# Packed steps of a fused four-layer block: probabilities turned by VectorE and through memory instead of by TensorE

## The chip, the cores and the metric

The program runs on one core of a Trainium2 chip. The core has five engines with a queue of their own each: TensorE (PE, matrix products; its weight loads are listed as PEld), VectorE (DVE), ScalarE (ACT), GpSimd (POOL) and SyncE (SP), which here only issues transfers. Engines wait for one another through semaphores, and each runs its instructions strictly in the order written. The metric is the device time in microseconds of one execution; lower is better.

## The reference

Four layers act on x (4 batches of 512 rows of 512), with a context of 4 x 512 x 256:

```
x = x + tanh(g_xattn[0]) * L0_xattn(layernorm(x), ctx)    # one head, softmax of q k^T over 512 keys
x = x + tanh(g_ffn[0])   * L0_ffn(layernorm(x))           # one 512 x 512 layer, weights from bits
x = x + tanh(g_xattn[1]) * L1_xattn(layernorm(x), ctx)    # 16 heads of 128
x = x + tanh(g_ffn[1])   * L1_ffn(layernorm(x))           # 16 experts, each row goes to 4

L1_xattn:  q = rmsnorm(h @ Wq)   k = rmsnorm(c @ Wk)   v = c @ Wv         (per head)
           out = softmax(q k^T / sqrt(128)) @ v ;  result = concat(out) @ Wo
L1_ffn:    for every expert: down( silu(gate(x)) * up(x) ), weighted by topk_weight
```

## The kernel before

**Precision.** Every product is made of three: each operand is split into a rounded part (`_hi`) and the rest (`_lo`), and lo x hi, hi x hi and hi x lo are added up in one PSUM bank (`product`, L505 to L507). Each split costs a ScalarE cast (`copy_hi`) and a subtraction on VectorE or GpSimd (`lower`).

**The steps.** After a first part (layers L0, up to about 150 us) the kernel runs steps t = 0 to 65. There are 64 items, each a (head, batch) of L1_xattn: first the 16 heads of batch 0, then for each head batches 1 to 3. Step t works on three items at a time: it projects keys, values and queries of item t, makes scores and probabilities of item u = t-1, and values and output projection of item w = t-2. When batch 0 is through its attention, its expert layer runs as 31 blocks of 128 rows (b = t - 20). Steps 20 to 50 carry one block each beside their attention work: these are the **packed** steps. A block needs three weight chunks: gate and up in two halves of 704 KB (`gate_up_weights`) and down in 768 KB (`down_weights`).

**Probabilities.** The four score tiles of an item (128 queries x 512 keys each) lie in two score banks by turns. VectorE takes the row maximum (`maximum`), scales it (`shift`), ScalarE takes the exponential into `prob` (`softmax`). The product with the values needs keys on the partitions, so each tile is turned: four TensorE transposes with the identity (`probs`, L573), into PSUM, then a cast (`probs_hi`) and a subtraction (`probs_lo`) write `probT`.

**Orders.** Nothing is scheduled by a program: each engine's `step(t)` is a list of calls in order. SP's list of a packed step is: second gate-up chunk (waits until the down product of the block before is through), store of that block's result, down chunk (waits for `gate_up(0)`), the weights of the next head if there is one (two steps in three), then the expert number of the next block by a load into a register, and that block's first gate-up chunk (waits for `gate_up(1)`).

```
for t in range(NI + 2):                       # SP
    ...
    if 0 <= b < NB - 1:
        e = expert(b + 1)
        gate_up_weights(b + 1, 0, e)          # first work of ScalarE in step t+1
```

## Time and profile before

| | us |
|---|---|
| three runs | 1462.48, 1463.65, 1465.13 (median 1463.65) |
| profiled execution, span from first to last instruction | 1461.5 |
| what lies around the span (median less span) | 2.15 |
| one packed step (PE's turn of `h_row`: 93 transposes, 3 a step, from 509.9 to 1214.6 us) | about 23.5 |
| PE busy | 1437.8 (98%) |
| DVE, ACT, POOL busy | 1107.0, 977.5, 864.5 |
| packets of the DMA queues | 55495, 142.74 MB, mean 98 GB/s |

The profiled execution has no time of its own in the record beside its span; the median stands for it. A packed step is read off by windows of 23.48 us that begin at the first score product (581.87, 605.35, 628.83 us).

### The profile page before, as it was taken

What the parts mean: (1) busy time and instruction counts of PE and PEld (TensorE: products, weight loads), DVE (VectorE), ACT (ScalarE), POOL (GpSimd) and SP (SyncE); (2) the same over time, 40 slices, a digit from 0 to 9 for tenths busy, and PEclk for the clock granted to TensorE, in tenths of its full rate; (3) what the DMA queues carried; (4) which work ended last, traced back from release to release, by engine and by line L of the source; (5) the groups of instructions that cost most, each with busy time, mean ns of one, the idle gap of its engine ahead of it and who ended that gap; (6) DMA issues with size and microseconds to landing.
All of it is one profiled execution on the core that took longest, in us unless ns stands there. A gap on an engine that the chain in (4) does not pass through costs nothing.

```text
span 1461.5 us, 23763 instructions
## 1 busy us (share of the span) xinstructions
PE 1437.8 (98%) x8086; PEld 1223.0 (84%) x8086; DVE 1107.0 (76%) x2100; ACT 977.5 (67%) x2224; POOL 864.5 (59%) x701
## 2 busy tenths in 40 slices
PE   8999999999999999999999999999999999999998
PEld 6778788888888888888888888888888888888887
DVE  7888777777777777777777777777777776787777
ACT  7864477777776667667676767667676765666664
POOL 4785555555554566666575757575666655664341
PEclk9999999999999999999999999999999999999999
DMA  8420011111111333434333433433434331321002
GB/s 325 159 66 16 22 44 45 57 44 44 44 44 44 139 124 126 149 108 147 124 129 127 139 123 127 139 117 132 136 115 144 125 126 36 107 82 37 8 1 87
DMA packets 55495, 142.74 MB, mean 98 GB/s; under 512 B 5392, under 2 KB 5392, under 8 KB 55376
## 3 DMA queue, kind: packets, MB, share of 16 engines
q1 hardware_dynamic: 51616, 128.90, 26.1%
q0 software_dynamic: 3760, 12.32, 3.0%
q8 instruction: 66, 1.08, 0.3%
q14 instruction: 53, 0.43, 0.1%
HBM read 126.79 MB, written 14.42 MB: 97 GB/s over the span
## 4 chain that ended last, share of the span: by engine, by line
PE 82%; DVE 7%; ACT 4%; POOL 4%; issue 2%; DMA 0%; ACTq 0%; SPq 0%; DVEq 0%; POOLq 0%
PE w_bank L505 10%; PE w_bank L507 10%; PE w_bank L506 10%; PE j_bank L505 9%; PE j_bank L507 9%; PE j_bank L506 9%; PE t_bank L573 7%; PE s_bank L505 4%; PE s_bank L507 4%; PE s_bank L506 4%; PE t_bank L538 2%; POOL q_scale L1855 2%; POOL wo_lo L1815 2%; ACT prob L927 1%; PE t_bank L657 1%
## 5 line engine op out<-in xcount | busy, mean ns | idle before, releaser
L927 ACT ACTIVATE prob<-s_bank,neg_bias,q_scale 128x512 f32<-128x512 f32 x255 | 198.0, 777 | 186.5 <-DVE neg_bias L1422 186.4
L1262 DVE TENSOR_TENSOR probT_lo<-t_bank,probT_hi 128x512 fp32r<-128x512 f32 x260 | 176.4, 689 | 168.4 <-ACT probT_hi L892 168.4
L1476 DVE SCALAR_TENSOR_TENSOR x_sb<-w_bank,inv_sum,x_sb 128x512 f32<-128x512 f32 x254 | 188.4, 744 | 0.0
L1401 DVE TENSOR_REDUCE neg_max<-s_bank 128x1 f32<-128x512 f32 x255 | 168.6, 682 | 0.9 <-PE s_bank L507 0.9
L1815 POOL TENSOR_TENSOR xnT_lo<-xnT_raw,xnT_hi 128x512 fp32r<-128x512 f32 (+2 forms) x47 | 126.5, 2693 | 61.5 <-ACT xnT_hi L892 61.5
L573 PE MATMUL t_bank<-ident,prob 128*128 128x128 f32 x1008 | 151.4, 273 | 1.3 <-ACT prob L927 1.1
L892 ACT CAST probT_hi<-t_bank 128x512 fp32r<-128x512 f32 x260 | 150.1, 590 | 1.8 <-PE t_bank L515 1.8
L1855 POOL TENSOR_TENSOR q_scale<-q_ss,minus_half 128x4 f32<-128x4 f32 x64 | 65.9, 1030 | 143.6 <-DVE q_ss L1414 143.6
L505 PE MATMUL j_bank<-wkv_lo,cT_hi 128*128 128x256 f32 x512 | 145.1, 283 | 0.7 <-DVE oT_lo L1262 0.4
L507 PE MATMUL j_bank<-wkv_hi,cT_lo 128*128 128x256 f32 x512 | 144.6, 282 | 0.0
L506 PE MATMUL j_bank<-wkv_hi,cT_hi 128*128 128x256 f32 x512 | 144.4, 282 | 0.0
L1815 POOL TENSOR_TENSOR sqs_lo<-xn,sqs_hi 128x512 fp32r<-128x512 f32 x62 | 80.6, 1300 | 104.2 <-ACT xn L1007 104.2
L1815 POOL TENSOR_TENSOR cT_round<-cT_raw,x_round 128x1408 fp32r<-128x1408 f32 (+1 forms) x31 | 104.5, 3371 | 58.8 <-ACT x_round L892 58.8
L573 PEld LDWEIGHTS t_bank<-ident,prob 128*128 128x128 f32 x1008 | 121.6, 140 | 20.9 <-ACT prob L927 2.6
L505 PE MATMUL w_bank<-wo_lo,oT_hi 128*128 128x512 f32 x254 | 112.5, 443 | 2.6 <-POOL wo_lo L1815 0.4
L892 ACT CAST oT_hi<-j_bank 128x512 fp32r<-128x512 f32 x64 | 37.0, 578 | 113.2 <-PE j_bank L507 113.2
L505 PE MATMUL s_bank<-kv_lo,qT_hi 128*128 128x512 f32 x255 | 110.1, 432 | 0.3 <-DVE kv_lo L1496 0.2
L505 PE MATMUL j_bank<-xnT_lo,wq_hi 128*128 128x512 f32 x256 | 108.5, 424 | 0.0
L505 PEld LDWEIGHTS j_bank<-wkv_lo,cT_hi 128*128 128x128 f32 x512 | 97.3, 190 | 9.3 <-DVE oT_lo L1262 3.6
L507 PE MATMUL j_bank<-xnT_hi,wq_lo 128*128 128x512 f32 x256 | 101.1, 395 | 0.0
L506 PEld LDWEIGHTS j_bank<-wkv_hi,cT_hi 128*128 128x128 f32 x512 | 97.4, 190 | 4.3
L507 PE MATMUL s_bank<-kv_hi,qT_lo 128*128 128x512 f32 x255 | 100.6, 395 | 0.0
(308 smaller groups left out, 4454.2 us busy)
## 6 DMA issues: line engine op xcount, KB each, us to landing
stage<-w SPq DMA_DIRECT2D x96, 256.0 KB, 3.4
xnT_raw<-w_gu SPq DMA_DIRECT2D x31, 704.0 KB, 4.8
cT_raw<-w_gu SPq DMA_DIRECT2D x31, 704.0 KB, 4.7
xnT_raw<-w_dn SPq DMA_DIRECT2D x16, 768.0 KB, 4.4
cT_raw<-w_dn SPq DMA_DIRECT2D x15, 768.0 KB, 4.7
planes<-bits SPq DMA_DIRECT2D x16, 512.0 KB, 4.8
y<-stage SPq DMA_DIRECT2D x31, 256.0 KB, 4.0
x_sb<-x SPq DMA_DIRECT2D x5, 1024.0 KB, 10.9
```

The lines of the kernel that those rows point to most:

```text
L505: pe.matmul(dst, lh, rl, start=first, stop=False)
L506: pe.matmul(dst, lh, rh, start=False, stop=False)
L507: return pe.matmul(dst, ll, rh, start=False, stop=last)
L538: last = pe.transpose(t_bank[0][:, j * P:(j + 1) * P], kv_raw[:, j, 0:HD], ident[:])
L573: last = pe.transpose(prob_bank(t, i)[:, j * P:(j + 1) * P], prob[:, i, j * P:(j + 1) * P], ident[:])
L892: return nc.scalar.copy(dst, src)
L927: nc.scalar.activation(prob[:, i, :], score_bank(t, i)[:], ACT.Exp, bias=neg_bias[:, u % 2, i:i + 1], scale=q_scale[:, u % 2, i:i + 1], ac ...
L1262: return nc.vector.tensor_tensor(dst, src, hi, ALU.subtract)
L1401: nc.vector.tensor_reduce(neg_max[:, u % 2, i:i + 1], score_bank(t, i)[:], AX_X, ALU.max, negate=True).then_inc(own_max, 1)
L1476: nc.vector.scalar_tensor_tensor(out=here, in0=w_bank[0][:] if packed else out_bank(t, i)[:], scalar=inv_sum[:, w % 2, i:i + 1], in1=here, ...
L1815: return nc.gpsimd.tensor_tensor(dst, src, hi, ALU.subtract)
L1855: nc.gpsimd.tensor_tensor(q_scale[:, u % 2, :], q_ss[:, u % 2, :], minus_half[:], ALU.pow).then_inc(q_scale_ready, 1)
```

## The change

In the packed steps (and only there: `moved(u)`) TensorE no longer turns the probabilities. Instead, for each pair of tiles (128 x 1024):

- ScalarE writes the exponentials in blocks of 32 keys (`rearrange("p (r j c) -> p j r c")`);
- VectorE transposes every 32 x 32 block in place (`turn_quads`, one instruction for a pair);
- SP stores the pair to device memory (512 KB in runs of 2 KB), waits for the store, and loads it back with four transfers of 128 KB, each onto 32 partitions, in runs of 512 bytes (`move_pair`);
- ScalarE casts (`moved_hi`) and VectorE subtracts (`moved_lo`) 128 x 1024 from SBUF to SBUF instead of four times 128 x 512 from PSUM.

Pair 0 is split at the end of the step, pair 1 at the head of the next. The third score tile gets a bank of its own (t_bank[1]), and the orders of all engines in a packed step are new. In all steps `probT` lies in another order (query blocks of 32 by key tiles), which the value products read with a two-level pattern.

```diff
+            def move_pair(u, pair):                                   # SP
+                if not moved(u):
+                    return
+                sp.wait_ge(p_quads[pair], MOVES[u] + 1)
+                wait(sp, p_moved[pair], 16 * NT * MOVES[u])
+                sp.dma_start(turn_dram[pair].rearrange("i p m -> p i m"), prob_pair(pair)).then_inc(p_stored[pair], 16)
+                sp.wait_ge(p_stored[pair], 16 * (MOVES[u] + 1))
+                for c in range(NT):
+                    sp.dma_start(
+                        prob_pair(pair)[c * QUAD:(c + 1) * QUAD].rearrange("a i (r m) -> a (i r) m", r=NT),
+                        turn_dram[pair].rearrange("i (r a) (c m) -> c a (i r) m", r=NT, c=NT)[c]).then_inc(
+                            p_moved[pair], 16)
...
                 if t >= H + 2 and fresh(t - 2):
                     out_weights(SET[t - 2] + 1)
+                move_pair(t - 1, 0)
+                move_pair(t - 1, 1)
                 if 0 <= b < NB - 1:
                     e = expert(b + 1)
                     gate_up_weights(b + 1, 0, e)
...
                 def values():                                         # PE
-                    need(pe, p_lo, 4, w, 4)
+                    wait(pe, p_lo, TILES[w + 1])
+                    if moved(w):
+                        pe.wait_ge(pair_lo[0], MOVES[w + 1])
+                        pe.wait_ge(pair_lo[1], MOVES[w + 1])
...
+                def moved_hi(v, pair):                                # ACT
+                    if not moved(v):
+                        return
+                    act.wait_ge(p_moved[pair], 16 * NT * (MOVES[v] + 1))
+                    need(act, pv_mm, 1, v - 1, 1)
+                    copy_hi(probT_pair(0, pair), prob_pair(pair)).then_inc(pair_hi[pair], 1)
...
                 gate_up_hi(0)
                 rows_to_hi()
+                moved_hi(w, 1)
...
+                    moved_hi(u, 0)
+                    query_squares()
+                    return
...
+                def turn_quads(pair):                                 # DVE
+                    if not moved(u):
+                        return
+                    need(dve, p_exp, 4, u, 2 * pair + 2)
+                    both = prob_pair(pair).rearrange("p i s -> p (i s)")
+                    nc.vector.transpose(both, both).then_inc(p_quads[pair], 1)
+
+                def moved_lo(v, pair):
+                    if not moved(v):
+                        return
+                    dve.wait_ge(pair_hi[pair], MOVES[v] + 1)
+                    lower(probT_pair(1, pair), prob_pair(pair), f32(probT_pair(0, pair))).then_inc(pair_lo[pair], 1)
...
+                    query_lo()
+                    key_lo()
+                    add(2)
+                    inner_lo()
+                    moved_lo(u, 0)
+                    add(3)
+                    return
```

SP, one packed step from the store of the last block's result to the next block's first chunk. `turn` is the new buffer in device memory, `block_expert` the table of expert numbers. Before:

```order
L447 DMA y<-stage 128x512 [waits y_copied]
L442 ISA [waits a_mm]
L442 DMA cT_raw<-w_dn 128x2x768
L411 DMA stage<-w 128x512 [waits wo_lo]
L427 TENSOR_LOAD block_expert
L427 ISA x2
L437 ISA [waits b_mm]
L437 DMA xnT_raw<-w_gu 128x1408
```

And now, from the down chunk on:

```order
L496 DMA xnT_raw<-w_dn 128x1536
L451 DMA stage<-w 128x512 [waits wo_lo]
L472 DMA turn<-prob 128x2x512 [waits p_moved0,p_quads0]
L475 DMA prob<-turn 32x8x128 [waits p_stored0]
L475 DMA prob<-turn 32x8x128 x3
L472 DMA turn<-prob 128x2x512 [waits p_moved1,p_quads1]
L475 DMA prob<-turn 32x8x128 [waits p_stored1]
L475 DMA prob<-turn 32x8x128 x3
L481 TENSOR_LOAD block_expert
L481 ISA x2
L491 ISA [waits b_mm]
L491 DMA cT_raw<-w_gu 128x2x704
```

Between the head's weights and the next block's expert number stand ten more transfers and four more waits, two of them for stores to land.

ScalarE, from the end of a packed step to the exponentials of the next. `xnT_raw` or `x_round` here hold a gate-up chunk, `routes` the inner rows of the block. Before:

```order
L892 CAST routes<-w_bank 128x384 [waits d_mm,h_turned]
L1005 ACTIVATE sqs_hi<-j_bank 128x512 [waits q_ss_mm,q_lo]
L1007 ACTIVATE xn<-j_bank 128x512 [waits q_ss_out]
L892 CAST probT_hi<-t_bank 128x4x128 [waits p_turned]
L892 CAST xnT_hi<-xnT_raw 128x1408 [waits a_in]
L892 CAST xnT_hi<-w_bank 128x512 [waits b_mm,q_mm,rows_mm]
L892 CAST wo_hi<-stage 128x512 [waits w_mm,wo_in]
L892 CAST oT_hi<-j_bank 128x512 [waits w_mm,pv_mm]
L927 ACTIVATE prob,row_sum<-s_bank,neg_bias,q_scale 128x512 [waits p_turned,s_max] x2
```

And now:

```order
L967 CAST routes<-w_bank 128x384 [waits d_mm,h_turned]
L967 CAST probT_hi<-prob 128x1024 [waits pv_mm,p_moved0]
L1095 ACTIVATE sqs_hi<-j_bank 128x512 [waits q_ss_mm,q_lo]
L1097 ACTIVATE xn<-j_bank 128x512 [waits q_ss_out]
L967 CAST xnT_hi<-xnT_raw 128x1408 [waits a_in]
L967 CAST xnT_hi<-w_bank 128x512 [waits b_mm,q_mm,rows_mm]
L967 CAST probT_hi<-prob 128x1024 [waits pv_mm,p_moved1]
L967 CAST wo_hi<-stage 128x512 [waits w_mm,wo_in]
L967 CAST oT_hi<-j_bank 128x512 [waits w_mm,pv_mm]
L1009 ACTIVATE prob,row_sum<-s_bank,neg_bias,q_scale 128x4x4x32 [waits pair_lo0,s_max] x2
```

The cast of the first gate-up chunk (`waits a_in`) still opens the step, and the new cast of pair 1 stands behind it.

VectorE, the end of a packed step. Before:

```order
L1496 SCALAR_TENSOR_TENSOR kv_lo<-t_bank,gain,kv_hi 128x512 [waits kT_hi]
L1476 SCALAR_TENSOR_TENSOR x_sb<-w_bank,inv_sum,x_sb 128x512 [waits w_mm]
L1262 TENSOR_TENSOR qT_lo<-j_bank,qT_hi 128x512 [waits q_hi]
L1262 TENSOR_TENSOR routes<-w_bank,routes 128x384 [waits h_hi]
L1476 SCALAR_TENSOR_TENSOR x_sb<-w_bank,inv_sum,x_sb 128x512 [waits w_mm]
L1262 TENSOR_TENSOR probT_lo<-t_bank,probT_hi 128x4x128 [waits p_hi]
```

And now:

```order
L1352 TENSOR_TENSOR qT_lo<-j_bank,qT_hi 128x512 [waits q_hi]
L1600 SCALAR_TENSOR_TENSOR kv_lo<-t_bank,gain,kv_hi 128x512 [waits kT_hi]
L1580 SCALAR_TENSOR_TENSOR x_sb<-w_bank,inv_sum,x_sb 128x512 [waits w_mm]
L1352 TENSOR_TENSOR routes<-w_bank,routes 128x384 [waits h_hi]
L1352 TENSOR_TENSOR probT_lo<-prob,probT_hi 128x1024 [waits pair_hi0]
L1580 SCALAR_TENSOR_TENSOR x_sb<-w_bank,inv_sum,x_sb 128x512 [waits w_mm]
```

The addition of the third output tile now comes behind both the query's and the key's low part, and the subtraction of pair 0 stands ahead of the last addition.

## Rows read from the trace of the kernel before

**Rows 1.** The page's busy times of all engines (us, share of the span, instructions).
```profile
PE 1437.8 (98%) x8086; PEld 1223.0 (84%) x8086; DVE 1107.0 (76%) x2100; ACT 977.5 (67%) x2224; POOL 864.5 (59%) x701
```
**Rows 2.** Window of one step: length, busy time of PE, PEld, DVE, ACT, POOL, granted clock, DMA share, GB/s.
```profile
581.87:605.35 23.48, 23.48 (x138) 20.60 (x138) 17.42 (x33) 16.17 (x36) 14.84 (x10) 1.00 0.38 126
```
**Rows 3.** The chain of waits, 580 to 640 us: start, length in us, engine and tile.
```profile
592.60 0.44 PE t_bank L573 x4
...
604.28 0.44 PE t_bank L573 x4
```
**Rows 4.** Timeline of PE: start, length, line, operation; values, gate-up, first turn.
```profile
586.37 0.39 PE L505 MATMUL j_bank<-probT_lo,kv_hi 128*128 128x512 f32 x1
590.52 0.33 PE L505 MATMUL w_bank<-xnT_lo,xnT_hi 128*128 128x352 f32 x1
592.43 0.60 PE L573 MATMUL t_bank<-ident,prob 128*128 128x128 f32 x4
```
**Rows 5.** Timeline of SP, its issues in and just ahead of packed steps.
```profile
480.21 0.38 SPq L469 DMA_DIRECT2D rows<-x_sb  x1
481.75 0.36 SPq L437 DMA_DIRECT2D xnT_raw<-w_gu  x1
592.77 0.34 SPq L442 DMA_DIRECT2D xnT_raw<-w_dn  x1
601.61 0.55 SPq L437 DMA_DIRECT2D cT_raw<-w_gu  x1
616.84 1.07 SPq L411 DMA_DIRECT2D stage<-w  x2
```
**Rows 6.** DMA issues (KB each, us to landing); windows from 457, 586 and 608 us.
```profile
x<-x_sb SPq DMA_DIRECT2D x1, 1024.0 KB, 4.3
stage<-w SPq DMA_DIRECT2D x1, 256.0 KB, 2.7
cT_raw<-w_gu SPq DMA_DIRECT2D x1, 704.0 KB, 4.8
y<-stage SPq DMA_DIRECT2D x1, 256.0 KB, 6.0
```
**Rows 7.** Timeline of ACT: chunk cast, row cast, value cast, first exponential of the step.
```profile
583.29 1.39 ACT L892 CAST xnT_hi<-xnT_raw 128x1408 fp32r<-128x1408 f32 x1
584.57 0.60 ACT L892 CAST xnT_hi<-w_bank 128x512 fp32r<-128x512 f32 x1
589.29 0.59 ACT L892 CAST oT_hi<-j_bank 128x512 fp32r<-128x512 f32 x1 [3.60 <-PE j_bank L507]
590.81 0.78 ACT L927 ACTIVATE prob<-s_bank,neg_bias,q_scale 128x512 f32<-128x512 f32 x1 [0.93 <-DVE neg_bias L1422]
```
**Rows 8.** Timelines of DVE and POOL: two-input operations on SBUF, alone and side by side.
```profile
41.75 0.74 DVE L1788 SCALAR_TENSOR_TENSOR kv_raw<-stage,bit_w,kv_raw 128x512 f32<-128x512 f32 x1
46.39 2.35 DVE L1788 SCALAR_TENSOR_TENSOR kv_raw<-stage,bit_w,kv_raw 128x512 f32<-128x512 f32 x1
585.25 1.61 DVE L1262 TENSOR_TENSOR xnT_lo<-xnT_raw,xnT_hi 128x1408 fp32r<-128x1408 f32 x1
45.77 2.42 POOL L1815 TENSOR_TENSOR cT_lo<-x_sb,cT_hi 128x1024 fp32r<-128x1024 f32 x1
601.82 3.51 POOL L1815 TENSOR_TENSOR xnT_lo<-xnT_raw,xnT_hi 128x1536 fp32r<-128x1536 f32 x1
```
**Rows 9.** Windows of 1 us around a pause of PE, columns as in rows 2.
```profile
50.00:51.00 1.00, 0.00 (x0) 0.00 (x0) 0.82 (x2) 1.00 (x5) 0.92 (x2) 1.00 0.77 289
52.00:53.00 1.00, 1.00 (x5) 0.77 (x4) 0.00 (x0) 0.90 (x1) 1.00 (x1) 0.61 0.00 0
53.00:54.00 1.00, 1.00 (x4) 0.81 (x3) 0.90 (x1) 0.00 (x0) 1.00 (x2) 0.50 0.03 10
54.00:55.00 1.00, 1.00 (x3) 0.79 (x3) 1.00 (x2) 0.12 (x1) 1.00 (x2) 0.50 0.68 240
55.00:56.00 1.00, 1.00 (x4) 0.77 (x3) 0.97 (x2) 1.00 (x2) 1.00 (x2) 0.68 0.93 289
```

More of the change, by code:

```diff
@@ L123, with moved, turned_tiles, flamingo_kernel @@
 LAST = {b: max(t for t in range(NI) if ITEMS[t][1] == b) for b in range(B)}
-def flamingo_kernel(nc, x, xT, ctxT, vecs, w0, bits, w1, w_gu, w_dn, topk_idx, topk_w, x0_dram, rows_dram, y_dram, out):
+QUAD = 32
+def moved(u):
+    return T0 <= u + 1 < T0 + NB
+def turned_tiles(u):
+    return () if moved(u) else range(NT)
+TILES = [sum(len(turned_tiles(v)) for v in range(u)) for u in range(NI + 1)]
+MOVES = [sum(moved(v) for v in range(u)) for u in range(NI + 1)]
+def flamingo_kernel(nc, x, xT, ctxT, vecs, w0, bits, w1, w_gu, w_dn, topk_idx, topk_w, x0_dram, rows_dram, y_dram, turn_dram, out):
     x_tiles = x.rearrange("(b i p) d -> b p i d", b=B, p=P)
@@ L320, in flamingo_kernel @@
             sem("s_mm"), sem("s_max"), sem("p_exp"), sem("p_turned"), sem("p_hi"), sem("p_lo"))
+        p_quads, p_stored, p_moved, pair_hi, pair_lo = (
+            [sem(f"{name}{pair}") for pair in range(2)] for name in ("p_quads", "p_stored", "p_moved", "pair_hi", "pair_lo"))
         late_normed, late_turned, late_hi, late_lo = (
@@ L534, in turn_keys @@
                     need(pe, q_ss_out, 1, 0, 1)
+                elif moved(t - 1):
+                    need(pe, q_ss_out, 1, t - 1, 1)
                 elif t:
-                    need(pe, p_lo, 4, t - 1, 2)
+                    wait(pe, p_lo, TILES[t - 1] + 2)
                 for j in range(NT):
@@ L556, in scores @@
                         need(pe, kT_lo, 1, u, 1)
-                    need(pe, p_exp, 4, u, (0, 0, 0, 1)[i] if t == LAST_SCORES else i - 1)
+                    if moved(u):
+                        need(pe, p_exp, 4, u, (0 if moved(u - 1) else -1, 0, 0, 1)[i])
+                        if i == 2 and not moved(u - 1):
+                            wait(pe, p_lo, TILES[u])
+                    elif moved(u - 1):
+                        need(pe, p_exp, 4, u, max(i - 1, 0))
+                    else:
+                        need(pe, p_exp, 4, u, (0, 0, 0, 1)[i] if t == LAST_SCORES else i - 1)
                     product(score_bank(t, i)[:], [a[:, u % 2, i * P:(i + 1) * P] for a in qT],
@@ L661, in table @@
                     pe.wait_ge(place_ready, 1 + NT)
-                    need(pe, p_lo, 4, 0, 4)
+                    wait(pe, p_lo, TILES[1])
                     for c in range(PAIRS):
@@ L793, in step @@
                 gate_up(0)
+                if moved(u):
+                    scores(3)
+                    key_value(1)
+                    project_out(0)
+                    query((0, 1))
+                    project_out(1)
+                    gate_up(1)
+                    query((2, 3))
+                    key_turn()
+                    project_out(2)
+                    turn_inner()
+                    project_out(3)
+                    return
                 probs(0)
@@ L925, in softmax @@
                     need(act, s_max, 4, u, i + 1)
[L926 to L927 removed]
+                    if i in turned_tiles(u - 1):
+                        wait(act, p_turned, TILES[max(u - 1, 0)] + list(turned_tiles(u - 1)).index(i) + 1 if u else 0)
+                    else:
+                        act.wait_ge(pair_lo[i // 2], MOVES[u])
+                    dst, src = prob[:, i, :], score_bank(t, i)[:]
+                    if i not in turned_tiles(u):
+                        dst = dst.rearrange("p (r j c) -> p j r c", j=NT, c=QUAD)
+                        src = bank_keys(score_bank(t, i))
+                    nc.scalar.activation(dst, src, ACT.Exp,
                                          bias=neg_bias[:, u % 2, i:i + 1], scale=q_scale[:, u % 2, i:i + 1],
@@ L1656, in step @@
                 take(1)
-                if not packed:
-                    values_lo()
+                values_lo()
                 if t == T0 - 1:
@@ new lines, in step @@
+                probs_lo(0)
+                maximum(2)
+                shift(2)
+                if t == T0 - 2:
+                    statistics(0, 1, NMOMENTS + 1)
+                if t == T0 - 1:
+                    nc.vector.memset(h_row[:, I:], 0.0).then_inc(pad_ready, 1)
+                take(2)
+                values_rows()
+                add(0)
+                maximum(3)
+                shift(3)
+                late_lower()
+                if t == T0 - 2:
+                    statistics(0, 2, NMOMENTS + 2)
+                    statistics(0, 3, NMOMENTS + 3)
+                    for i in range(NT):
+                        mean_variance(0, i, NMOMENTS + i)
@@ L1715, in _ @@
+                take(3)
+                probs_lo(1)
+                probs_lo(2)
+                query_lo()
+                add(1)
+                key_lo()
+                if t == NI - 1:
+                    last_squares_lo()
+                probs_lo(3)
+                add(2)
+                if not deferred(t):
+                    add(3)
             for kind, b in DVE_ORDER:
@@ L2066 @@
     x0 = nc.dram_tensor("x0", (S, D), F32, kind="Internal").ap()
-    flamingo_kernel(nc, *args, x0, rows, y, out)
+    turn = nc.dram_tensor("turn", (2, 2, P, S), F32, kind="Internal").ap()
+    flamingo_kernel(nc, *args, x0, rows, y, turn, out)
     result = run_bass_kernel_spmd(nc, [arrays], core_ids=[0])
```

201 lines of the change are left out of this document (84 added, 117 removed).

## The prediction

> **What bounds the kernel now.** First the page's busy times: TensorE (PE) is busy for 98% of the span, the next engine for 76% [rows 1]. In the window of one packed step PE is busy for all of its 23.48 us at full clock, VectorE for 17.4, ScalarE for 16.2, GpSimd for 14.8, and the DMA engines for 0.38 of it [rows 2]. So before the change the step's length is the sum of PE's instructions, and nothing is waited for. Next the chain of waits, for what PE's probability turns are worth in it: each group of four takes 0.44 us there (0.36 to the next start, and the product after it starts 0.08 later than usual), and a step has four such groups [rows 3]. Then the timelines of PE, SP and ScalarE, to see when the transfers are asked for and when they are used.
>
> **What goes.** 4 x 0.44 = 1.76 us of PE in each of 31 packed steps, 54.6 us in all. If nothing else moved, a step would take 21.72 us and the kernel 1463.65 - 54.6 = 1409 us. The four casts and four subtractions of 128x512 become two each of 128x1024: about even. VectorE gains two block transposes.
>
> **What comes, and where it lies.** The cover for the transfers is the question, because SP does them in line. SP's list now has, between the down chunk and the next block's first gate-up chunk: store, wait for landing, four loads, store, wait for landing, four loads. That gate-up chunk is the first thing ScalarE casts in the next step; behind this cast in ScalarE's queue stand the row cast, the cast of pair 1, the value cast and all exponentials. The value products on PE need pair 1's low part, the exponentials need the value cast ahead of them, pair 0's transposes need two exponentials, and SP's first store needs the transposes. That closes a ring from one step's value products to those of the next. Its length, from the start of the value products:
>
> 1. To the first store's issue. Before, the down chunk is issued at 592.77 us, 6.4 after the value products start at 586.37 (rest of the values, keys, gate-up, which ends where the turn starts at 592.43) [rows 4, 5]. Its issue takes 0.34 to 0.56, and in two steps of three the head's weights follow (1.07 for two, half of that for one, so 0.5 on average) [rows 5]: 7.4 us. The transposes are ready by then: value products to value cast 2.9, cast 0.6, two exponentials 1.6 [rows 7], then one 128x1024 transpose. No row has such an operation; the nearest, 1408 elements in 1.61 us [rows 8], gives 1.2 by length: 6.3 in all. At half of that nothing changes; at twice it the transposes end 7.5 after the start, and the ring is 0.1 longer.
> 2. First store landing, 512 KB. Rows for it: 256 KB alone 2.7, 1024 KB alone 4.3, 256 KB queued behind a 704 KB chunk 6.0 [rows 6]. This store is queued behind the down chunk issued about 1 us earlier. I take 4.3, bounds 2.7 and 6.0.
> 3. Four loads issued: 0.35 to 0.56 each, 1.07 for two back to back [rows 5]: 2.1, bounds 1.4 and 2.8.
> 4. Second store: behind 512 KB of loads only, so between the two rows without a queue, 3.5; bounds 2.7 and 6.0. Its transposes are long done.
> 5. Four loads: 2.1, bounds as above.
> 6. The expert number is loaded into a register behind all this instead of in SP's idle time. Between the issue at 480.21 (0.38 long) and the one at 481.75 lie such a load and its address: 1.2 at most [rows 5]. I take 1.1, lower bound 0.
> 7. Gate-up chunk landing: 4.8 [rows 6]. The last loads of pair 1 land before it and are hidden.
> 8. ScalarE's chunk cast, 1.28 to the next start, row cast 0.5, cast of pair 1 about 1.0 (by length from the 1.39 for 1408), then VectorE's subtraction, about 1.2 (from 1.61) [rows 7, 8]: 4.0.
>
> Sum 7.4 + 4.3 + 2.1 + 3.5 + 2.1 + 1.1 + 4.8 + 4.0 = 29.3 us. All lower bounds at once (7.0 + 2.7 + 1.4 + 2.7 + 1.4 + 0 + 4.8 + 4.0) still give 24.0, above 23.48; all upper ones (7.7 + 6.0 + 2.8 + 6.0 + 2.8 + 1.2 + 4.8 + 4.0) give 35.3.
>
> 9. PE now waits for 5 to 8 us ahead of the value products. After its pause from about 49.1 to 51.2 us the granted clock stood at 0.61, 0.50, 0.50 and 0.68 of full in the four windows from 52 to 56 us (0.50 is the lower level, 1.2 GHz), which loses 0.39 + 0.5 + 0.5 + 0.32 = 1.7 us of work [rows 9]. The longer pause before each step's value products should bring the same, and it falls in item 1. I add 1.7, bounds 0 and twice that.
>
> 31.0 us a step against 23.48. The ring closes over the 30 passages between the 31 packed steps: 30 x 7.5 = 226 us; the step that is left over brings about its 1.8 us of gain, which I leave out. Against the profiled execution: span 1461.5 + 226 = 1687.5, and 2.15 us around it: 1689.6, by the median 1463.65 the same; call it 1689.
>
> **Costed at nothing.** The additions and low parts in a new order on VectorE: the third addition now waits for query and key low parts, and the last output product of PE waits for it. From the end of the query products 0.6 (cast) + 0.7 + 0.7 + 0.7 = 2.7 us pass, while PE has about 1.5 of other work: 1.2 us of wait, but PE is idle in the ring anyway. The new layout in all other steps (runs of 32 elements in casts, subtractions and value products): no row shows such runs; the 0.33 for 128x352 products and the casts of 1408 [rows 4, 7] are of contiguous data, so a tenth on 12 value products of 0.23 in some 33 steps, 9 us, bounds it from above, and nothing from below. Room in the DMA engines: 2 MB more a step on 3 MB; from 0.38 of 23.48 us busy to about 0.5 of 31, no limit by itself.
>
> **A shared port.** A two-input operation of VectorE on SBUF took 0.74 us alone and 2.35 when it began at 46.39 beside GpSimd's operation of 45.77 to 48.19: it ended 0.6 after that one had ended, as if it had been held until then [rows 8]. The two new subtractions are of this kind, and that of pair 0 falls on GpSimd's 3.51 us for the down chunk, ahead of the last addition, for which the next step's down product waits. The Trainium skill says the same (SBUF — State Buffer, section "SBUF: two separate sides"): the port pair is an exclusive lock, held for a whole instruction. By that rule, and the trace agrees, up to 3 us of VectorE are lost per step; in the ring it is hidden behind the chunk's landing, without the ring it would decide (rival 2).
>
> **Rivals.**
> - **Rival 1, slow loads (10%).** A load reaches 32 partitions only, in runs of 512 bytes; no row has either. If one takes 1.2 us of the DMA engines and not the 0.27 of the slope from 256 KB in 2.7 to 1024 KB in 4.3 [rows 6], four take 4.8, not hidden by 2.1 of issuing: 2.7 more for each pair, 36.4 a step, 1463.65 + 30 x 12.9 = 1851 us. For it: the four new transfers are unlike any row. Against: the same bytes. The Trainium skill (SBUF — State Buffer, "Door 1: The DMA port swizzle") states that partitions 0 to 31 reach 8 of 16 ports and half the bandwidth; by it a load would take about 0.6 us, an estimate from that page, and the step some 0.5 more. No run here shows it.
> - **Rival 2, transfers hidden, VectorE's order decides (4%).** If both round trips shrink so that the ring is under 23 us, the waits of the third addition (1.2) and part of the held subtraction (1.1) remain: 21.72 + 2.3 = 24.0, or 1463.65 + 30 x 0.5 = 1479. Against: every transfer row.
> - **Rival 3, the other side: the change does what it removes (4%).** PE stays the bound at 21.72: 1409 us, or some 1430 with one of the waits. It decides from the point where items 2 to 7 take less than 21.7 - 11.4 = 10.3 us instead of 17.9: both stores must land in some 1.5 us and the chunk in under 4. The fastest row of any transfer is 2.7.
> - **No change (1%)**: ring at 23.4 to 23.6 by chance.
>
> **How the numbers follow.** Forecast 81%, 1689 us. Its own spread: stores a microsecond faster each, issues at 0.4 and no clock loss give 27.2 a step, 1575; a microsecond slower each and twice the clock loss 34.7, 1800. Rival 1 lies above this range, rivals 2 and 3 below, and with the tails of the forecast some 20% are left out. Faster by over 0.2% (3 us, about what a measurement of this kernel can tell from none): 4%; within: 1%; slower: 95%.
>
> **What the profile will show.** PE's busy share falls to near 83% (1383 of some 1687), its longest wait by far being the value products (L505, `j_bank`) for VectorE's `probT_lo`, 5 to 8 us a step; ScalarE's chunk cast of the gate-up waits 5 us for the transfer; the issue of the store `turn` follows the down chunk by about 1 us and lands after 3 to 5; the granted clock dips at the value products. It is wrong if steps stay under 25 us (the round trips overlap more than SP's list says), if the first wait of the step is for pair 1's own landing (rival 1), or if PE waits at the down product and the last output product only (rival 2).

## The result and the profile after

The changed kernel takes 1752.4 us (median of four, 1748.4 to 1757.2) against 1463.2 for the kernel before (four, 1462.5 to 1465.1): ratio 1.197, 95% interval 1.195 to 1.200. Forecast were 1689 us, range 1575 to 1800, slower with 0.95. The sign and the range held; the loss is 289 us where 226 were worked out. The profiled execution has a span of 1750.3 us. A packed step, taken between the first and the last turn of `h_row` (510.8 and 1500.0 us), is 989.2 / 30 = 32.97 us long, against about 23.5 before; 30 x 9.5 is 284 of the 289 us. Where a mean is given below for a part of a step, it is over the 29 steps whose value products start between 525.6 and 1447.8 us, read from the trace's timelines in the same way as the step shown.

The page of the changed kernel, busy us, share of the span and instructions of each engine, which answers to [rows 1], and the line of the DMA queues:

```profile
PE 1473.6 (84%) x7590; PEld 1227.1 (70%) x7590; DVE 1174.8 (67%) x2100; ACT 979.7 (56%) x2162; POOL 853.1 (49%) x701
DMA packets 139814, 207.73 MB, mean 119 GB/s; under 512 B 10352, under 2 KB 73840, under 8 KB 139696
```

TensorE fell from 98% to 84%, with more busy us for less work: part of it ran at half clock. No engine took the bound over; the others fell in share too. What bounds the step is a chain through all of them and the transfers. SP's timeline of one step (start, length, line, operation), which answers to [rows 5]:

```profile
730.93 0.55 SPq L496 DMA_DIRECT2D cT_raw<-w_dn  x1
731.53 0.60 SPq L451 DMA_DIRECT2D stage<-w  x1
732.23 0.37 SPq L472 DMA_DIRECT2D turn<-prob  x1
738.59 1.80 SPq L475 DMA_DIRECT2D prob<-turn  x4
740.49 0.40 SPq L472 DMA_DIRECT2D turn<-prob  x1
743.98 1.78 SPq L475 DMA_DIRECT2D prob<-turn  x4
746.52 0.37 SPq L491 DMA_DIRECT2D xnT_raw<-w_gu  x1
```

The wait for a store is the stretch from its issue to the loads: 6.36 us for pair 0, 3.49 for pair 1, though both carry 512 KB between the same tensors. Over all packed steps pair 0 takes 5.8 to 6.5 us and pair 1 3.3 to 3.7. Ahead of the first, 768 KB of down weights and 256 KB of the head's weights went into the same queue 1.3 and 0.7 us earlier; ahead of the second only the loads back. Then ScalarE, VectorE and TensorE of the same step (in brackets: idle before, and what released it):

```profile
750.88 1.37 ACT L967 CAST xnT_hi<-xnT_raw 128x1408 fp32r<-128x1408 f32 x1 [5.53 <-DMA xnT_raw<-w_gu]
752.63 1.05 ACT L967 CAST probT_hi<-prob 128x1024 fp32r<-128x1024 f32 x1
```

```profile
752.28 1.63 DVE L1352 TENSOR_TENSOR xnT_lo<-xnT_raw,xnT_hi 128x1408 fp32r<-128x1408 f32 x1 [5.31 <-ACT xnT_hi L967]
753.82 1.22 DVE L1352 TENSOR_TENSOR probT_lo<-prob,probT_hi 128x1024 fp32r<-128x1024 f32 x1
```

```profile
722.79 0.77 PE L561 MATMUL j_bank<-probT_lo,kv_hi 128*128 128x512 f32 x1 [6.11 <-issue]
...
755.25 0.77 PE L561 MATMUL j_bank<-probT_lo,kv_hi 128*128 128x512 f32 x1 [5.86 <-issue]
```

The value products start 0.2 us after the low part of pair 1 ends, at 755.04. The record names "issue" and not VectorE as what released them; the order in time, and the fifth experiment, show that it is this low part. The last view is the clock (windows of 1 us, columns as in [rows 2]; the granted clock is the third number from the right), which answers to [rows 9]:

```profile
753.00:754.00 1.00, 0.00 (x0) 0.00 (x0) 1.00 (x2) 1.00 (x2) 0.00 (x0) 0.79 0.56 224
754.00:755.00 1.00, 0.00 (x0) 0.00 (x0) 1.00 (x2) 0.19 (x1) 0.00 (x0) 0.50 0.12 48
755.00:756.00 1.00, 0.75 (x2) 0.69 (x3) 0.96 (x3) 0.00 (x0) 0.00 (x0) 0.50 0.00 0
...
759.00:760.00 1.00, 1.00 (x4) 0.80 (x3) 0.14 (x2) 0.00 (x0) 0.00 (x0) 0.50 0.70 262
760.00:761.00 1.00, 1.00 (x7) 0.87 (x6) 0.00 (x0) 0.34 (x1) 0.00 (x0) 0.80 0.00 0
```

TensorE stopped at 749.4. The clock fell to its lower level (1.2 GHz) during the pause and stayed there for 5 us of work, so the twelve value products took 5.2 us (755.25 to 760.46). In experiment 1 below, where TensorE hardly pauses, they take 2.9 and the granted clock is full; in the kernel before they took 2.7.

### The profile page after: what moved, and what is told of

Its sections match the earlier page's. It is cut to its first block, busy times and chain, and to the rows that moved or that the text cites. A ratio compares the mean times of both kernels' runs of the same rounds, so it can differ in the third digit from the quotient of the medians.

```text
span 1750.3 us, 23049 instructions
## 1 busy us (share of the span) xinstructions
PE 1473.6 (84%) x7590; PEld 1227.1 (70%) x7590; DVE 1174.8 (67%) x2100; ACT 979.7 (56%) x2162; POOL 853.1 (49%) x701
## 2 busy tenths in 40 slices
DMA packets 139814, 207.73 MB, mean 119 GB/s; under 512 B 10352, under 2 KB 73840, under 8 KB 139696
## 4 chain that ended last, share of the span: by engine, by line
PE 53%; DMA 16%; issue 13%; DVE 8%; ACT 4%; SPq 4%; POOL 2%; ACTq 0%; DVEq 0%; POOLq 0%
DMA turn<-prob 11%; PE j_bank L561 8%; PE j_bank L562 8%; PE j_bank L563 8%; PE w_bank L561 6%; PE w_bank L563 5%; PE w_bank L562 5%; DMA prob<-turn 5%; PE t_bank L639 3%; DVE probT_lo L1352 3%; SPq L475 2%; ACT probT_hi L967 2%; PE s_bank L561 2%; DVE x_sb L1580 2%; PE s_bank L563 2%
## 5 line engine op out<-in xcount | busy, mean ns | idle before, releaser
L561 PE MATMUL j_bank<-probT_lo,kv_hi 128*128 128x512 f32 (+1 forms) x256 | 131.3, 513 | 180.6 <-issue 180.3
L1009 ACT ACTIVATE prob<-s_bank,neg_bias,q_scale 128x512 f32<-128x512 f32 x224 | 174.5, 782 | 166.8 <-DVE neg_bias L1512 166.7
L561 PEld LDWEIGHTS j_bank<-probT_lo,kv_hi 128*128 128x128 f32 x256 | 63.1, 247 | 208.1 <-issue 192.8
L1352 DVE TENSOR_TENSOR probT_lo<-t_bank,probT_hi 128x512 fp32r<-128x512 f32 x136 | 91.0, 688 | 84.8 <-ACT probT_hi L967 84.8
L1491 DVE TENSOR_REDUCE neg_max<-s_bank 128x1 f32<-128x512 f32 x224 | 147.2, 681 | 0.9 <-PE s_bank L563 0.9
L967 ACT CAST xnT_hi<-xnT_raw 128x1408 fp32r<-128x1408 f32 (+2 forms) x63 | 76.1, 1217 | 92.2 <-DMA xnT_raw<-w_gu 87.4
L562 PE MATMUL j_bank<-probT_hi,kv_hi 128*128 128x512 f32 (+1 forms) x256 | 125.6, 490 | 0.0
L563 PE MATMUL j_bank<-probT_hi,kv_lo 128*128 128x512 f32 (+1 forms) x256 | 124.5, 487 | 0.0
L967 ACT CAST x_round<-cT_raw 128x1408 fp32r<-128x1408 f32 (+1 forms) x46 | 65.0, 1414 | 105.7 <-DMA cT_raw<-w_gu 95.8
L1352 DVE TENSOR_TENSOR probT_lo<-prob,probT_hi 128x1024 fp32r<-128x1024 f32 x62 | 76.1, 1227 | 48.3 <-ACT probT_hi L967 48.2
```

What stands on the lines that cost most here:

```text
L561: pe.matmul(dst, lh, rl, start=first, stop=False)
L562: pe.matmul(dst, lh, rh, start=False, stop=False)
L563: return pe.matmul(dst, ll, rh, start=False, stop=last)
L967: return nc.scalar.copy(dst, src)
L1009: nc.scalar.activation(dst, src, ACT.Exp, bias=neg_bias[:, u % 2, i:i + 1], scale=q_scale[:, u % 2, i:i + 1], accum_out=row_sum[:, u % 2, ...
L1352: return nc.vector.tensor_tensor(dst, src, hi, ALU.subtract)
```

## The experiments

**1. Without the transfers.** The stores and loads are left out; ScalarE's casts wait for the block transposes. The value products then use tiles that are turned only inside blocks of 32; the exchange between the partitions is left out with the transfers.

```
-                move_pair(t - 1, 0)
-                move_pair(t - 1, 1)
...
-                    act.wait_ge(p_moved[pair], 16 * NT * (MOVES[v] + 1))
+                    act.wait_ge(p_quads[pair], MOVES[v] + 1)
```

> Left out: the stores of the turned probabilities and the loads that bring them back, so the value products of packed steps use tiles that are turned only inside blocks of 32. Everything else (block transposes, new order, casts, third score bank, layout) stays. Ring theory: the whole loss is in the ring through SyncE's transfers; without them the ring is about 11.4 us and another limit takes over, PE's 21.7 us a step or VectorE's order at 24.0: 1409 to 1479 us, the gate-up chunk's issue back in SyncE's idle time, no pause of PE above 1.5 us. Rival theory (the order of the step itself is bad, transfers only show it): 1550 us or more, with PE still waiting 3 us or more at one place of each step.

Measured: 1483.6 us against 1464.5, ratio 1.013 (1.011 to 1.014). A step is 24.1 us (`h_row`, 510.8 to 1234.1 us, by 30). The transfers and what hangs on them are 1752.4 - 1483.6 = 269 of the 289 us. The other 19 are the order's own: TensorE, by its waits between 600 and 1030 us (total, times, longest):

```profile
PE w_bank L559 <- DVE x_sb L1578: 22.6, 18, 1.3
PE j_bank L559 <- issue: 10.9, 18, 1.0
```

The first is the last output product waiting for the third addition, 1.26 us a step; the second is the value products, 0.6. So even free transfers would have left the change, with this order, slower than the kernel before.

**2. The layout alone.** The kernel before with runs of 32 in the casts, subtractions and value products.

```
-                    copy_hi(probT[0][:, :, i * P:(i + 1) * P],
-                            prob_bank(t, i)[:].rearrange("p (j q) -> p j q", j=4))
+                    copy_hi(probT_tile(0, i), bank_keys(prob_bank(t, i)))
...
-                                       [a[:, j, :] for a in probT], j == 0, j == NT - 1)
+                                       [a[:, j] for a in probT_keys], j == 0, j == NT - 1)
```

> The kernel before with one part of the change alone: the new order of columns in the turned probabilities (runs of 32), in the casts, subtractions and value products of all steps; turns, order and banks as before. The prediction bounded this by +9 us from above and nothing from below. If runs of 32 cost TensorE or the casts nothing: 1463.5, within 0.2%. If they cost a tenth of the value products everywhere (66 steps x 12 x 0.023): +18 us.

Measured: 1468.6 us, ratio 1.0030 (1.0016 to 1.0044), 4 us. The value products take 400 ns where they took 389 (groups by shape, 560 to 1160 us), the casts and subtractions the same as before; 12 x 0.011 = 0.13 us a step, and 31 x 0.13 = 4 us.

**3. The first store ahead of the down chunk.**

```
+                store_pair(t - 1, 0)
                 if 0 <= b < NB:
                     down_weights(b, e)
...
-                move_pair(t - 1, 0)
-                move_pair(t - 1, 1)
+                load_pair(t - 1, 0)
+                store_pair(t - 1, 1)
+                load_pair(t - 1, 1)
```

> Only SyncE's order changes: the store of pair 0 is issued ahead of the down chunk and of the head's weights, the wait for it and its loads stay behind them. In the trace that store took 6.3 us behind the 704 KB chunk, the like store of pair 1 3.5 us with nothing ahead. Queue theory: the store lands in about 3.5 us and is issued 1 us earlier, but the chunk now stands between it and its loads and the second store, which may land up to 1 us later: 3 to 4 us a step less, 1632 to 1662 us. Rival theory (the first store is slow by itself, for its place in memory or for the clock): only the earlier issue counts, 1 us a step, 1722 us.

Measured: 1663.7 us, ratio to before 1.136 (1.134 to 1.138): 89 us less than the changed kernel, 3.0 a step, 2 us above the queue theory's range and far from the rival's 1722. SP's timeline of one step:

```profile
713.14 0.37 SPq L472 DMA_DIRECT2D turn<-prob  x1
713.70 0.55 SPq L501 DMA_DIRECT2D cT_raw<-w_dn  x1
714.30 0.65 SPq L451 DMA_DIRECT2D stage<-w  x1
716.33 1.80 SPq L480 DMA_DIRECT2D prob<-turn  x4
718.23 0.39 SPq L472 DMA_DIRECT2D turn<-prob  x1
723.07 1.78 SPq L480 DMA_DIRECT2D prob<-turn  x4
```

The same store that landed after 6.4 us now lands after 3.2 (713.14 to 716.33; 3.1 to 3.5 over all steps). The weights have not gone: pair 1's store, now behind them, lands after 4.2 us in the mean where none of the head's tensors was queued, 5.3 where one was and 5.9 where two were. In the mean of a step the two landings together take 8.3 us for 9.7, and the first store's issue comes 8.4 us after the value products start and not 9.9; so about half of the 3.0 us is the weights' delay, now partly overlapped with the first store, and half is the earlier issue, which the expectation had put at 1 us.

**4. The chunk between the pairs.**

```
                 move_pair(t - 1, 0)
-                move_pair(t - 1, 1)
                 if 0 <= b < NB - 1:
                     e = expert(b + 1)
                     gate_up_weights(b + 1, 0, e)
+                move_pair(t - 1, 1)
```

> Only SyncE's order changes: register load and issue of the next gate-up chunk stand between pair 0's loads and pair 1's store. Ring theory with the queue: the chunk arrives 5.3 us earlier, but pair 1's store stands behind 704 KB and takes 6.3 us, then loads 1.8, their landing 2.7, cast and subtraction 2.3; from the start of the value products 9.5 + 6.3 + 1.9 + 1.1 + 6.3 + 1.8 + 2.7 + 2.3 = 31.9 us a step against 33.0: some 1720 us, and PE's pause now ends by pair 1's own landing. Rival theory (the chunk's way alone is what costs, pair 1 has 5 us to spare): 27.7 a step, 1592 us.

Measured: 1756.5 us, 4 us over the changed kernel, with intervals that overlap (1.197 to 1.201 against 1.195 to 1.200 of before). Nothing is won by taking the chunk's whole way out of the chain, since pair 1 takes its place. SP, and ScalarE's cast of pair 1:

```profile
744.02 0.37 SPq L491 DMA_DIRECT2D xnT_raw<-w_gu  x1
744.50 0.39 SPq L472 DMA_DIRECT2D turn<-prob  x1
750.48 1.79 SPq L475 DMA_DIRECT2D prob<-turn  x4
752.46 0.57 SPq L491 DMA_DIRECT2D cT_raw<-w_gu  x1
```

```profile
757.40 1.04 ACT L967 CAST probT_hi<-prob 128x1024 fp32r<-128x1024 f32 x1 [6.36 <-DMA prob<-turn]
```

Pair 1's store takes 6.0 us behind the chunk where it took 3.5, and its last load lands at 757.4, 5.6 us after its issue (2.7 in the median elsewhere), beside the second half of the gate-up weights. The forecast of 1720 had left that last delay out.

**5. TensorE kept busy in the pause.**

```
+                    need(pe, v_lo, 1, w, 1)
+                    need(pe, kv_second, 1, min(u, NI - 1), 1)
+                    for n in range(44 if moved(w) and moved(u) else 0):
+                        pe.transpose(j_bank[0][:, n % 4 * P:(n % 4 + 1) * P], ident[:], ident[:])
                     if moved(w):
                         pe.wait_ge(pair_lo[0], MOVES[w + 1])
                         pe.wait_ge(pair_lo[1], MOVES[w + 1])
-                    need(pe, v_lo, 1, w, 1)
-                    need(pe, kv_second, 1, min(u, NI - 1), 1)
```

> The changed kernel, with 44 transposes of the identity into the bank of the value products, issued by TensorE in its pause ahead of these products (some 0.11 us each, 4.8 of the 6 us). The products overwrite them; nothing else changes. In the trace the clock is granted at half for the twelve value products and they take 5.1 us and not 2.6. Clock theory: the pause makes the clock fall, the loss lies in the ring, and with the pause filled a step is 2.4 us shorter: 1752 - 30 x 2.4 = 1680 us. Rival: the clock at the value products is off the path, or falls for another reason: 1745 to 1755 us.

Measured: 1700.3 us, ratio to before 1.159 (1.155 to 1.163): 52 us less than the changed kernel. TensorE, then the first whole window of 1 us after the value products' start:

```profile
743.54 4.97 PE L650 MATMUL j_bank<-ident 128*128 128x128 f32 x44
749.54 0.48 PE L561 MATMUL j_bank<-probT_lo,kv_hi 128*128 128x512 f32 x1 [1.03 <-DVE probT_lo L1354]
```

```profile
750.00:751.00 1.00, 1.00 (x6) 0.80 (x5) 0.97 (x2) 0.00 (x0) 0.19 (x1) 1.00 0.00 0
```
With the pause filled the clock is at full here and the value products take 2.9 us (749.54 to 752.48). So it is in 25 of 29 steps; in four they still take 4.2 to 5.3. The gain is 1.7 us a step where 2.4 was expected, because the expectation took the loss from one step: in the mean the value products take 4.96 us in the changed kernel and 3.15 here, 1.8 less. That arrives in the ring: the store of pair 0 is issued 8.1 us after the value products start and not 9.9. With TensorE awake the record also names what it waited for: `probT_lo`.

**6. The weights issued by ScalarE.** SyncE's list loses the three chunks and the register load; ScalarE issues them from its own queue.

```
                 moved_hi(w, 1)
                 if packed:
+                    chunk_load(b, 1)
...
                     gate_tanh(0)
+                    chunk_load(b, 2)
                     softmax(2)
...
                     gate_tanh(1)
+                    chunk_load(b + 1, 0)
```

> The three chunks of the expert's weights and the register load of its number are issued by ScalarE, in its own queue: gate-up halves after the casts of pair 1 and after the second tanh, down chunk after the first tanh. SyncE keeps the stores, the loads back and the small transfers. List theory (the ring is long because SyncE does all in line, and because stores stand behind a chunk in its queue): store 0 is issued 6.7 us after the value products start, lands in 3.5, loads 1.8, store 1 3.5 to 6.3, loads 1.8, landing 2.7, cast and subtraction 2.3: 22.4 to 26.7 us a step, with the order's own floor of 24.0: 1485 to 1580 us, best guess 1530, and the chunk off the path. Rival theory (the transfers themselves or the memory are the limit, whichever queue they are in: 1.9 us for the DMA engines' work on a store and as much for its loads, beside 4.5 for the chunks): 1690 us or more.

Measured: 1580.4 us, ratio to before 1.076 (1.071 to 1.081): 172 us less than the changed kernel, 5.7 a step, at the upper edge of the list theory's range; the rival is out. Steps alternate between some 25 and 29 us. SP in a short step and in the long one behind it, then ScalarE's issues of chunks that fall beside these stores:

```profile
746.24 0.38 SPq L472 DMA_DIRECT2D turn<-prob  x1
749.52 1.97 SPq L475 DMA_DIRECT2D prob<-turn  x4
751.59 0.40 SPq L472 DMA_DIRECT2D turn<-prob  x1
755.52 1.78 SPq L475 DMA_DIRECT2D prob<-turn  x4
...
770.28 0.37 SPq L472 DMA_DIRECT2D turn<-prob  x1
776.22 1.80 SPq L475 DMA_DIRECT2D prob<-turn  x4
778.12 0.40 SPq L472 DMA_DIRECT2D turn<-prob  x1
784.85 1.78 SPq L475 DMA_DIRECT2D prob<-turn  x4
```

```profile
746.30 0.57 ACTq L973 DMA_DIRECT2D cT_raw<-w_dn  x1
...
770.26 0.40 ACTq L973 DMA_DIRECT2D xnT_raw<-w_dn  x1
...
777.60 0.56 ACTq L968 DMA_DIRECT2D cT_raw<-w_gu  x1
```

What shortened the step is the list. Of the 5.7 us, 3.4 lie behind pair 1's store, where register load, chunk issue and chunk landing no longer stand in line (8.1 us to the next value products for 11.5, in the mean). Another 2.6 lie ahead of pair 0's store (issued 7.3 us after the value products start for 9.9), 1.4 of it by the clock: the value products take 3.6 us in the mean for 5.0.

The stores themselves did not get faster in the mean: 5.0 us (3.1 to 8.1) against 4.9 (3.3 to 6.5) in the changed kernel. But this mean is over two kinds. In the short steps they land after 3.3 us (746.24) and 3.9 (751.59). In the long ones pair 0's store lands after 5.9 us (770.28) beside a down chunk, and pair 1's after 6.7 (778.12) behind a gate-up chunk that ScalarE had issued 0.5 us earlier. So a chunk that is issued from another queue at the same moment or just ahead slows a store as much as one in its own queue. The Trainium skill (DMA: Bandwidth & Descriptors, section "Queues, rings and completion order") says that the DMA engines take turns between the queues by packets; the long steps agree. Why pair 0's store keeps its 3.3 us in the short steps, where the down chunk is issued only 0.06 us after it, stays open.

**7. One load instead of four.** The blocks of 32 are not exchanged between the partitions then; that part of the transposition is left out.

```
-                for c in range(NT):
-                    sp.dma_start(
-                        prob_pair(pair)[c * QUAD:(c + 1) * QUAD].rearrange("a i (r m) -> a (i r) m", r=NT),
...
+                sp.dma_start(prob_pair(pair), turn_dram[pair].rearrange("i p m -> p i m")).then_inc(p_moved[pair], 16)
```

> Each pair comes back in one transfer of 512 KB over 128 partitions in runs of 2 KB and not in four of 128 KB over 32 partitions in runs of 512 bytes; the blocks are not exchanged between partitions then, so that part of the transposition is left out. Forecast's view (the four cost their issue, 1.8 us against 0.4, on SyncE, and nothing else): 2 x 1.4 = 2.8 us a step less, 1668 us. Rival 1 of the prediction (narrow loads are slow in the DMA engines): more than that, 4 to 8 us less, 1510 to 1630 us, and the DMA engines' busy share falls by a tenth or more. If the issue of one such transfer isn't shorter either, 1752.

Measured: 1745.7 us, ratio to before 1.191 (1.188 to 1.193), 7 us less than the changed kernel: neither theory. SP:

```profile
737.83 0.37 SPq L474 DMA_DIRECT2D prob<-turn  x1
738.29 0.41 SPq L472 DMA_DIRECT2D turn<-prob  x1
743.63 0.36 SPq L474 DMA_DIRECT2D prob<-turn  x1
```

The issue is 1.4 us shorter, and the second store, now right beside its pair's load, lands after 5.3 us where it took 3.5. From the first load's issue to the second store's landing it is 5.8 us here and 5.4 (738.59 to 743.98) with four loads. The issue of four was no cost of its own: it lay beside the transfer. Behind pair 1 the same holds for the chunk: from the loads' first issue to the chunk's it is 1.1 us for 2.6, but the chunk then lands after 5.6 us for 4.5 (means). Narrow loads, four together, are not slower either: the DMA engines' share in the packed stage is 0.49 with four and 0.50 with one, with 139814 and 89221 packets in all. The half bandwidth that the Trainium skill (SBUF — State Buffer, section "Door 1: The DMA port swizzle") states for partitions 0 to 31, weighed in rival 1, does not show. It is not refuted: the four are issued 0.45 us apart and reach all 128 partitions between them, and no run times one by itself.

**8. Only pair 0 through memory.** The order and banks of before; tiles 2 and 3 stay on TensorE. SyncE stores the pair behind the down chunk and loads it back behind the head's weights.

```
+def turned_tiles(u):
+    return (2, 3) if moved(u) else (0, 1, 2, 3)
...
                 if packed:
+                    turn_quads()
                     inner(0)
...
                 probs_hi(3)
+                moved_hi(u)
...
                     probs_lo(3)
+                    moved_lo(u)
```

> The order of before on TensorE, ScalarE and VectorE, two score banks, and only tiles 0 and 1 of a packed step turned by the block transpose and memory; tiles 2 and 3 by TensorE as before. SyncE: store behind the down chunk and the head's weights, four loads, then the next gate-up chunk. Ring theory: counted from the start of the value products, with the changed kernel's measured parts, store issued at 7.9, landed 14.3, last load landed 18.5, cast 19.6, low part 20.8, where 23.5 are to be had; the gate-up chunk arrives at 21.5, used at 27. So all is hidden and TensorE loses two of its four groups of turns (four were worth 1.48 us of its busy time a step without the transfers, so 0.74), 31 x 0.74 = 23 us less, 4 us more for the layout: 1446 us, 1.3% under the kernel before. Rival theory (any round trip through memory costs more than turns do, since VectorE's and ScalarE's queues are held by the cast and the low part of the pair): one wait of 1 us or more a step on TensorE, 1475 us or more.

Measured: 1476.6 us, ratio 1.009 (1.007 to 1.011), the rival's side. The round trip is hidden: no wait for a load is among the waits. But the pair's low part stands in VectorE's queue ahead of the maxima and the squares. ScalarE, then TensorE (in brackets the wait):

```profile
592.89 0.78 ACT L984 ACTIVATE prob<-s_bank,neg_bias,q_scale 128x512 f32<-128x512 f32 x1 [2.29 <-DVE neg_bias L1488]
```

```profile
593.81 0.50 PE L546 MATMUL s_bank<-kv_lo,qT_hi 128*128 128x512 f32 x1 [0.48 <-ACT prob L984]
```

Every step now takes 23.87 us: a shorter ring (squares, scale, shifts, exponential, score product) has become the bound.

**9. The squares first.** One change in VectorE's order.

```
                     gate_up_lo()
+                    squares_out()
                     rows_to_lo()
                     copy_y()
-                    squares_out()
-                    inverses()
-                    values_lo()
                     shift(0)
                     shift(1)
+                    inverses()
+                    values_lo()
```

> The kernel of e8 with one change in VectorE's order: the query squares stand ahead of the rows' low part and the y copy, and the two shifts ahead of the inverses and the values' low part. In e8 the transfers were hidden, but a step took 23.87 us: the pair's low part (1.23) on VectorE pushed the squares back, ScalarE waited 2.3 us for the shifts before its first exponential, and TensorE 0.5 for that exponential at the third score product. Order theory: the shifts come 1 us earlier, the wait is gone, and TensorE's own work decides, 23.5 - 0.7 + 0.1 = 22.9 us a step: 1476.6 - 30 x 0.97 = 1447 us, faster than before by 1%. Rival theory (waits of that size only move to the next place, since VectorE and ScalarE now work on paths without slack): 23.5 us or more, 1465 to 1477.

Measured: 1439.5 us (median of five, 1438.2 to 1440.9) against 1464.3, ratio 0.983 (0.982 to 0.984). This is the fastest kernel of all, 25 us under the one before. Its page, ScalarE's first exponential, and SP:

```profile
PE 1415.2 (98%) x7838; PEld 1198.5 (83%) x7838; DVE 1144.9 (80%) x2100; ACT 976.5 (68%) x2193; POOL 887.6 (62%) x701
```

```profile
589.71 0.78 ACT L984 ACTIVATE prob<-s_bank,neg_bias,q_scale 128x512 f32<-128x512 f32 x1 [1.09 <-DVE neg_bias L1488]
```

```profile
592.64 0.37 SPq L454 DMA_DIRECT2D turn<-prob  x1
...
598.36 1.80 SPq L461 DMA_DIRECT2D prob<-turn  x4
```

TensorE has no wait in packed steps and a step takes 22.69 us. Against the 23.61 of the layout alone that is 0.92 for two groups of turns, a little over their 0.44 each. The store lands after 5.7 us here (4.7 to 6.2 over all steps), nearly as slowly as in the changed kernel, and costs nothing. Beside experiment 8 it is also a test of the queue: SyncE's list is the same in both, but the down chunk is issued 1.1 us ahead of the store here and 2.3 us there, where the store lands after 3.9 us in the mean (3.2 to 5.2).

**10. The same order on the kernel before, all turns on TensorE.** The edit is that of experiment 9.

> The kernel before with VectorE's new order of e9 alone (squares ahead of rows and y copy, shifts ahead of the inverses); all turns by TensorE, old layout. If e9's gain comes from the two groups of turns that TensorE no longer does, the order alone brings nothing where TensorE is busy all the time: 1460 to 1467 us. Rival: the order is the gain (TensorE's starts are packed more densely by it): under 1450 us.

Measured: 1464.4 us, ratio 1.0002 (0.9993 to 1.0011). The order alone brings nothing; it only uncovers what two groups of turns are worth.

## Why the prediction was right, and what it mis-sized

The mechanism was right: a ring from one step's value products to the next through SyncE's list. Its items, measured in the step that starts at 722.79 (from, to) and in the mean of 29 steps:

| item of the prediction | forecast us | this step us | from, to | mean us |
|---|---|---|---|---|
| 1 and 9, to the first store's issue, with the clock | 9.1 | 9.44 | 722.79, 732.23 | 9.86 |
| 2, first store | 4.3 | 6.36 | 738.59 | 6.27 |
| 3, four loads issued | 2.1 | 1.90 | 740.49 | 1.90 |
| 4, second store | 3.5 | 3.49 | 743.98 | 3.47 |
| 5 and 6, four loads, register load | 3.2 | 2.54 | 746.52 | 2.60 |
| 7, chunk landing | 4.8 | 4.36 | 750.88 | 4.48 |
| 8, casts and low parts | 4.0 | 4.37 | 755.25 | 4.38 |
| sum | 31.0 | 32.46 | | 32.97 |

- **Item 2 is the term that was mis-sized.** It took 4.3 between the rows of a transfer alone and the 6.0 of one behind a chunk, though it said itself that a chunk had been issued 1 us earlier. The nearest row was that 6.0, and the measured 6.3 is even over the upper bound. It is 2.0 us a step too low. The other items' errors cancel: item 1 is 0.8 longer and item 8 0.4, items 3, 5 to 7 together 1.1 shorter. So the sum is 2.0 short as well, 59 of the 63 us missing over 30 steps. Experiment 3 took the weights from ahead of this store, and it landed after 3.2 us.
- Items 3 and 5 were right in size and wrong in kind. The loads' issue is not a price by itself (experiment 7): the transfers beside it take as long.
- Item 8 left VectorE's gate-up subtraction out, which stands between ScalarE's cast of pair 1 and its low part: the low part starts at 753.82 and the cast has ended at 753.68: 0.1 us of the 0.4 that item 8 is longer. Another 0.2 is the stretch from the low part's end to the first product (755.04 to 755.25), which it left out too. Item 6 was 0.75 instead of 1.1, the block transpose 1.24 instead of 1.2.
- Item 9 was right as a place and nearly as a price: 1.7 was added, the value products take 2.0 us longer in the mean (4.96 against 2.93 in experiment 1), and experiment 5 won 1.7 a step. That is 0.3 of the 0.8 us that item 1 is longer; the rest was not followed.
- Two workings of the prediction do not come out. The lower end of its range: stores 2 us less, issues at 0.4 (1.0 less over both pairs) and no clock loss (1.7 less) give 26.3 us a step and 1548 us, not 27.2 and 1575. Rival 3's condition: two stores in 1.5 us each and a chunk in 4, with the issues and the register load as in its items, sum to 12.3 us and not to 10.3. Neither bears on the outcome, since the time lies in the upper half of the range.
- Costed at nothing: the third addition's wait, forecast 1.2, is 1.26 in experiment 1 and hidden in the ring, as said. The layout costs 4 us, inside its bound of 9.
- The shared port: in the changed kernel the pair-0 subtraction comes after GpSimd's down operation and takes 1.22 us; the forecast that it would be held was wrong there. It is true where they overlap. Without the transfers (experiment 1) VectorE and GpSimd show:

```profile
706.00 1.59 DVE L1350 TENSOR_TENSOR probT_lo<-prob,probT_hi 128x1024 fp32r<-128x1024 f32 x1
...
710.90 1.21 DVE L1350 TENSOR_TENSOR probT_lo<-prob,probT_hi 128x1024 fp32r<-128x1024 f32 x1
```

```profile
703.03 3.47 POOL L1915 TENSOR_TENSOR xnT_lo<-xnT_raw,xnT_hi 128x1536 fp32r<-128x1536 f32 x1
```

  The first began 0.5 us before GpSimd's ended and took 0.4 longer than the second. An effect of that kind, with the price of the overlap and not of the whole operation.
- Rival 1 is out (experiment 7). Rival 2 was right about what lies under the ring: forecast 24.0 a step and 1479 us, measured 24.1 and 1483.6; the layout's 4 us are most of the rest. Its terms were not all right: value products wait 0.6 where a held subtraction of 1.1 was put, and TensorE's own work is 22.2 us a step (396.46 busy of 430 us) where 21.72 was. Rival 3, the change doing what it removes, is not to be had with this order even with free transfers. A part of it is, 25 us, with half of the tiles and the order of before with the squares moved (experiment 9).
- Of the signs named beforehand: busy share 84% for 83; ScalarE's wait for the chunk about 6 us for 5; TensorE's pause 6.0 in the mean for 5 to 8; pair 0's store landing 5.8 to 6.5 for "3 to 5", the sign of the mis-sized term. The releaser was to be `probT_lo`; the record says "issue".

Steps vary between 31.9 and 34.5; that the mean is 0.5 over the step taken apart lies almost all in item 1 (9.86 against 9.44). Open: an order of the full change that hides both pairs was not tried.

## What to carry to other kernels

A round trip through memory has to fit the whole way around the ring it closes, with every wait in the issuing engine's list summed; here one pair of tiles fits a 23 us step, and two did not in any order tried. Size a transfer's landing by a row with the same neighbours in flight, not by the mean of rows with and without them. When a resource is relieved by moving half of a job away, look again at the order of the engine that took it over: the same kernel was 0.9% slower than the one before, and 1.7% faster with three calls moved.

## What was not expected of the hardware

- A 512 KB store to memory landed after 3.1 to 3.7 us with little beside it (pair 0 in experiment 3, pair 1 in the changed kernel) and after 5.8 to 6.5 with a 768 KB load issued 0.5 to 1.8 us ahead of it. With the load 2.3 us ahead it was 3.9 in the mean (experiment 8). A chunk issued from ScalarE's queue at the same moment or 0.5 us ahead slowed a store as much in every second step of experiment 6 (5.6 to 6.2 us and 5.9 to 8.1); in the others, with a down chunk issued 0.06 us after it, it took 3.3.
- Four loads of 128 KB into 32 partitions each, in runs of 512 bytes, cost the chain as much as one of 512 KB into 128 partitions: 5.4 against 5.8 us up to the next store's landing.
- In a pause of TensorE of 5.9 us the granted clock fell to half before work resumed and came back 5 us after it; 44 small transposes in the pause kept the value products at their full speed in 25 of 29 steps.
- Value products that read their right side in runs of 32 elements took 400 ns for 389.
